# A retention stage in fp32 on one core: three moves in the order of work (low part of the turned values, gate function, scores)

## The reference, cut to what matters

```
q, k = rope(x @ Wq), rope(x @ Wk)          # 8 heads of 128
v, g = x @ Wv, x @ Wg                      # 8 heads of 256
scores = (q * scale) @ k^T * D             # D: decay of the head, causal
o = scores @ v
o = o * rsqrt(mean(o*o) + eps) * g_norm_weight
o = o * silu(g)
x = layernorm(x + o @ Wo)
```

## Time and profile before

| | before |
|---|---|
| median of 3 runs (lowest to highest) | 2827.63 us (2826.35 to 2828.19) |
| the profiled execution: its own time | 2827.04 us |
| its span, first to last instruction | 2825.2 us |
| PE busy | 2757.8 us (98%) |
| DVE busy | 1586.9 us (56%) |
| ACT busy | 1104.8 us (39%) |
| mean granted clock of TensorE | 0.995 |
| PE's share of the chain that ended last | 91% |

### The profile page before, as it was taken

The page is one execution under the profiler, slowest core; times in us unless marked ns, Lnnn a source line. Parts: engine busy times, 40 slices in busy tenths (PEclk is TensorE's granted clock), DMA queues, the critical chain, the costliest instruction groups (busy, mean ns, idle before and its releaser), DMA issues.

```text
span 2825.2 us, 40399 instructions
## 1 busy us (share of the span) xinstructions
PE 2757.8 (98%) x15498; PEld 2506.3 (89%) x15498; DVE 1586.9 (56%) x2104; ACT 1104.8 (39%) x1718; POOL 28.8 (1%) x45
## 2 busy tenths in 40 slices
PE   8999999999999999999989999999999999999997
PEld 7888899888888888888878888889999998998997
DVE  3233222344454444467778888854884573673766
ACT  3333233332223223334457777742442241341432
POOL 0000000000000000000000000000000000000000
PEclk9999999999999999999999999999999999999999
DMA  5222332211111111104112222212211122121222
GB/s 179 84 84 87 102 100 92 84 62 47 58 54 50 45 53 51 60 32 105 60 66 67 72 66 72 66 47 90 79 60 67 55 74 75 53 74 55 75 89 93
DMA packets 88144, 203.51 MB, mean 72 GB/s; under 512 B 9476, under 2 KB 64260, under 8 KB 73832
## 3 DMA queue, kind: packets, MB, share of 16 engines
q1 hardware_dynamic: 88040, 202.09, 21.3%
HBM read 171.86 MB, written 30.21 MB: 72 GB/s over the span
## 4 chain that ended last, share of the span: by engine, by line
PE 91%; DVE 4%; ACT 2%; issue 1%; DMA 0%; SPq 0%; DVEq 0%; POOL 0%; ACTq 0%
PE PS L128 8%; PE PS L130 8%; PE PS L129 8%; PE PS L1957 5%; PE PS L1959 5%; PE PS L1961 5%; PE PS L1482 5%; PE PS L409 3%; PE PS L411 3%; PE PS L410 3%; PE PS L434 3%; PE PS L435 3%; PE PS L436 3%; PE PS L1495 3%; PE PS L1994 2%; PE PS L1993 2%
## 5 line engine op out<-in xcount | busy, mean ns | idle before, releaser
L128 PE MATMUL PS<-XH,WH 128*128 128x512 f32 (+1 forms) x1216 | 423.6, 348 | 4.7 <-ACT G L726 3.8
L130 PE MATMUL PS<-XH,WL 128*128 128x512 f32 (+1 forms) x1216 | 419.8, 345 | 0.0
L129 PE MATMUL PS<-XL,WH 128*128 128x512 f32 (+1 forms) x1088 | 373.7, 343 | 0.0
L88 ACT ACTIVATE WH<-RAW 128x1024 fp32r<-128x1024 f32 x106 | 112.3, 1060 | 499.0 <-PE PS L130 359.5
L94 DVE TENSOR_TENSOR WL<-RAW,WH 128x1024 fp32r<-128x1024 f32 x106 | 129.7, 1224 | 253.0 <-ACT WH L88 251.8
L128 PEld LDWEIGHTS PS<-XH,WH 128*128 128x128 f32 x1216 | 228.8, 188 | 32.2 <-ACT G L726 7.1
L130 PEld LDWEIGHTS PS<-XH,WL 128*128 128x128 f32 x1216 | 228.9, 188 | 25.7
L129 PEld LDWEIGHTS PS<-XL,WH 128*128 128x128 f32 x1088 | 204.5, 188 | 22.5
L2084 ACT ACTIVATE WH<-RAW 128x512 fp32r<-128x512 f32 x180 | 113.4, 631 | 225.7 <-PE PS L1961 118.6
L409 PE MATMUL PS<-CH,KWH 128*128 128x338 f32 (+1 forms) x512 | 168.1, 328 | 13.1 <-DVE CL L385 13.1
L2312 DVE TENSOR_TENSOR WL<-RAW,WH 128x512 fp32r<-128x512 f32 x196 | 134.7, 688 | 61.8 <-ACT WH L2084 59.2
(11 more groups left out here) (311 smaller groups left out, 6582.0 us busy)
## 6 DMA issues: line engine op xcount, KB each, us to landing
RAW<-weights_dram SPq DMA_DIRECT2D x111, 1024.0 KB, 4.9
a_KRAW<-keys_scratch SPq DMA_DIRECT2D x32, 411.0 KB, 3.1
a_VRAW<-values_scratch SPq DMA_DIRECT2D x32, 384.0 KB
R<-context_dram SPq DMA_DIRECT2D x8, 1352.0 KB, 6.8
R<-context_dram SPq DMA_DIRECT2D x7, 1536.0 KB, 7.0
values_scratch<-VS SPq DMA_DIRECT2D x40, 256.0 KB
keys_scratch<-KS SPq DMA_DIRECT2D x8, 768.0 KB, 5.9
keys_scratch<-KS SPq DMA_DIRECT2D x8, 676.0 KB, 5.7
```

What stands on the lines that cost most here:

```text
L128: pe.matmul(out, wh, xh[:, k, cols], start=(k == 0), stop=False)
L129: pe.matmul(out, wh, xl[:, k, cols], start=False, stop=False)
L130: mm = pe.matmul(out, wl, xh[:, k, cols], start=False, stop=(k == KT - 1))
```

## The change

Nothing is computed otherwise and no instruction of an engine is added or removed but register instructions. Three pieces of the order move:

1. Loop heads, DVE: `VL` stood between output additions 3 and 4 (behind a weight split) and now stands behind addition 7. PE's own order in the loop heads stays.
2. Heads 0 to 6, ACT: the gate function of gate unit 1 stood behind the weight split of the second unit of the next head; it now stands ahead of it and waits for `unit_done` itself, at the same count.
3. Heads 0 and 7: PE does the scores ahead of the transposes, and DVE masks the scores ahead of `VL`.

```diff
@@ scalar, head
                 if not end:
-                    weights_ahead(WG + 1, i, first)
+                    u, loop = unit_no(WG + 1, i, first)
+                    act.wait_ge(c.unit_done, 8 * loop + (u + 1 - U_RET))
                 else:
...
                 act.activation(halves(G[:, 1, :]), row800(c, 0), ACT.Silu).then_inc(gated, 1)
                 if end:
                     end_hi(3)
+                else:
+                    weights_ahead(WG + 1, i, first)
                 act.preload_act_table_set("natural_log_exp_and_others")
@@ vector, head
                 if not first and not end:
-                    for n in range(4):
+                    for n in range(KT):
                         add_output(n, i)
-                    weights_ahead(WO, i, first)
...
+                        if n == 3:
+                            weights_ahead(WO, i, first)
+                    turned_low(i)
+                    weights_ahead(WO + 1, i, first)
+                    mask_scores(i)
+                else:
+                    mask_scores(i)
+                    turned_low(i)
                 dve.wait_ge(s_hi, i + 1)
@@ tensor, head
                 if not first and not end:
                     project_output(i, range(4))
+                    turn(i)
                     project_output(i, range(4, KT))
...
                     pe.wait_ge(r_added, 8 * i - 1)
+                    scores(i)
 
                     pe.wait_ge(r_added, 8 * i)
+                else:
+                    scores(i)
+                    turn(i)
```

More of the change, by code:

```diff
@@ L807, in add_last, with turned_low @@
                 norm.add_row(dve, h, n, r_added, 8 * END - 8 + KT * h + n + 1)
-            def head(i, first):
-                end = i is END
-                rope(0, i, first, lambda: weights_ahead(0, i, first))
-                rope(1, i, first, lambda: weights_ahead(1, i, first))
-                for t in range(2):
-                    weights_ahead(WV + t, i, first)
-                if not first and not end:
-                    for n in range(4):
-                        add_output(n, i)
-                    weights_ahead(WO, i, first)
+            def turned_low(i):
                 dve.wait_ge(v_hi, i + 1)
@@ L824, in head, with mask_scores @@
                                   ALU.subtract).then_inc(v_lo, 1)
[L825 to L828, removed]
+            def mask_scores(i):
                 dve.wait_ge(s_raw, i + 1)
@@ L836, in head @@
                 ins.then_inc(s_masked, 1)
+            def head(i, first):
+                end = i is END
+                rope(0, i, first, lambda: weights_ahead(0, i, first))
+                rope(1, i, first, lambda: weights_ahead(1, i, first))
+                for t in range(2):
+                    weights_ahead(WV + t, i, first)
+                if not first and not end:
+                    for n in range(KT):
+                        add_output(n, i)
+                        if n == 3:
[6 more added lines that the diff above has]
+                    turned_low(i)
                 dve.wait_ge(s_hi, i + 1)
@@ L970, in project_last, with turn, scores @@
                     tile(HALF_BANKS[n % 4], 1, n, 1, False, True).then_inc(wo_last, 1)
+            def turn(i):
+                pe.wait_ge(v_kept, 2 * i + 2)
+                for t in range(2):
+                    mm = turn_values(c, pe, VT[:, t, :], 4, t * P, RDV)
+                mm.then_inc(v_turned, 1)
+            def scores(i):
+                pe.wait_ge(qk_lo, 2 * i + 2)
+                for b in range(B):
+                    out = c.PS[0:T, b // 4, (b % 4) * T:(b % 4 + 1) * T]
+                    cols = slice(b * T, (b + 1) * T)
+                    (qh, ql), (kh, kl) = QK
+                    pe.matmul(out, kh[:, cols], qh[:, cols], start=True, stop=False)
+                    pe.matmul(out, kh[:, cols], ql[:, cols], start=False, stop=False)
+                    mm = pe.matmul(out, kl[:, cols], qh[:, cols], start=False, stop=True)
+                mm.then_inc(s_raw, 1)
             def head(i, first):
@@ L1003, in head @@
                     project_output(i, range(4))
[L1005 to L1009, removed]
+                    turn(i)
                     project_output(i, range(4, KT))
-                pe.wait_ge(qk_lo, 2 * i + 2)
-                if not first and not end:
                     pe.wait_ge(r_added, 8 * i - 1)
[L1016 to L1024, removed]
+                    scores(i)
                     pe.wait_ge(r_added, 8 * i)
+                else:
+                    scores(i)
+                    turn(i)
                 weights(WG, i, first)
```

## The result

| | before | after |
|---|---|---|
| median in the comparison (lowest to highest) | 2826.99 us (2824.34 to 2828.19), 4 runs | 2809.47 us (2806.72 to 2811.43), 4 runs |
| ratio, 95% interval | | 0.9938 [0.9926, 0.995] |
| the profiled execution: time, span | 2827.04, 2825.2 us | 2811.43, 2809.6 us |
| PE busy | 2757.8 us | 2757.5 us |
| mean granted clock | 0.995 | 0.993 |

The changed kernel is faster, by 17.5 us where 15.5 were forecast. The median lies 0.03 us under the lower end of the range, 2809.5. The direction and the mechanism came out; the size was too small, and the lower end too near. Of the 2.6 us between the forecast 2812.1 and 2809.47, 2.0 are the larger saving; the other 0.6 is that the kernel before had a median of 2826.99 us in this comparison, where the forecast started from 2827.63.

What follows compares the result with a forecast made beforehand. PE, busy 98% of the span, was taken as the bound, with only its waits to gain. Savings of 6.5 + 4.7 + 4.3 = 15.5 us from 2827.63 gave 2812.1 us, range 2809.5 to 2817.0.

Steps and rivals of the forecast that it cites:

- Bound and mechanism: Whole kernel: PE busy 98% of the span; only its waits can shrink, 12.6 us idle at three places.
- Part 1: Six loop heads: with VL behind the additions, output tiles no longer wait for an addition; 6 x 1.09 = 6.5 us saved.
- The cover of the chain behind it: Loop heads, DVE from addition 7 to SL's end: 3.2 us to spare before PE asks for its results.
- Part 2: Seven head ends: with the gate function ahead of the split, Q starts sooner; 7 x 0.68 = 4.7 us saved.
- the baseline: Head 7: the sums-of-squares matmuls are followed without a wait after 1.45 us, taken as Q's turn at the other head ends.
- the spare time: Head ends: the moved gate function is done 0.4 us ahead of PE's turn for Q.
- Part 3: Heads 0 and 7: scores run inside the transposes' wait for the copy of V; 2 x 2.16 = 4.3 us saved.
- rival (d): Later seam of attention and feed-forward: the clock falls otherwise, 2.6 us either way, 2809.5 or 2814.7; no chance of its own.
- The sum: Whole kernel: 6.5 + 4.7 + 4.3 = 15.5 us saved, giving 2812.1 us, ratio 0.9945.
- (a): Any of the three places: one part gives its wait back to another waiter, 2816.4 to 2818.6 us; one part lost 0.15.
- (b): Six loop heads: VL's late place starves gate unit 1, each microsecond beyond the cover costs 6 us; slower 0.04.
- (c): The three places: register work or issue sets the waits, so no saving, 2827.6 us; within 0.2% 0.05.

Runs made afterwards that it cites:

- cover1: The changed kernel with VL written twice in the six loop heads (one more, about 2.3 us): 2809.4 us, one run.
- cover2: The changed kernel with VL written three times in the six loop heads (two more): 2819.71 us, one run.
- endgate: The changed kernel with head 7's gate function ahead of the third split of the last output weights: second output matmul at 1.52 us instead of 1.70.
- gatelate: The changed kernel with one more ScalarE copy (about 0.43 us) ahead of the gate function at seven head ends: 2813.13 us.
- part 3 alone: The kernel before with only scores ahead of transposes and mask ahead of VL in heads 0 and 7: 2823.24 us, ratio 0.9983.

## Why the prediction was right or wrong

**Bound and mechanism: right.** PE's waits were all there was to gain. All three went, nothing new took their place, and the blocks behind took the saving over.

**Part 1: right to 0.1 us** (6.5 forecast, 6.52 measured alone), with the step from VL's end to addition 4 as its evidence. The cover of the chain behind it was 3.1 us for 3.2 (cover1, cover2).

**Part 2: the mechanism right, the term too small**, 4.7 for 5.76 us. The step that failed is the baseline, "in head 7 the same four are followed without a wait after 1.45 us". They were not: PE's weight load there waited 0.55 us, and the gate function of head 7 held it (endgate). The list of PE's waits did not show it, because PE's matmul row was still counted as busy with the sums of squares; the row of the weight load did. By the second matmul the head 7 baseline was 1.71 us and Q's own is 1.57: 0.14 x 7 = 1.0 us. The row in front of the prediction speaks of four matmuls; the program has two there (line 1057, one for each half of the tokens), which the profile shows as four records. The same error made the spare time 0.4 us instead of 0.15 (gatelate). And a wait may be gone from the list while it still sets the start.

**Part 3: right in its fixed work** (4.3 forecast, 4.19 measured), incomplete in what a wait costs. The step that failed is in rival (d): I looked for falls of the clock only at one later seam where the trace of before had one, and took the wait of 1.93 us in heads 0 and 7 to cost its own length, since that one profile showed the clock at 1.00 there. In two of seven profiles the wait also costs a fall, 4.8 and 1.7 us, about 0.9 us per execution as a mean of these seven. That is a small sample, and part 3 alone took 4.06 us off the median, no more than its fixed work. That falls come behind this wait and cost time is shown; how often they come, and how the length of the wait changes that, is not.

**The sum.** 16.6 us of fixed work, and about 0.9 for falls that no longer come, make 17.5, which is what the comparison gave. With four runs of each, a spread of 4 to 5 us and a share of falls from seven profiles the agreement to 0.1 is luck; in the later sessions the changed kernel was 18.5 and 21.4 us under the kernel before.

**Profile against median.** The prediction had the saving right by the profiled executions (15.6 us) for a wrong reason: 16.6 were saved in the block and 1.0 was lost behind it, in a part of the span that varies from 1641.8 to 1646.6 us between profiles of the same kernel. The range had 2.6 us below the forecast for the clock, from half of one fall in a window of ten microseconds. A mean granted clock of 0.995 over 2825.2 us is some 28 us at the lower level (an estimate: 0.005 x 2825.2 / 0.5), and the part behind the block varied by 4.8 us, so the term was too small in itself; and the range had to hold an error in the sizes and in the starting median as well, and did not.

**The rivals.** (a) no part was lost; the loop's branch costs nothing that shows (part 2 gave 0.83 us per loop head). (b) real, but 3.1 us away. (c) no. (d) true of the later seams, where the term was too small, and missed in head 0.

## What to carry to other kernels

Before a row is taken as "what it costs without a wait", look at the weight load's row as well as the matmul's, and measure to the second matmul behind the place: a matmul that overlaps fp32 work ahead of it can hide a wait of some tenths. A wait of PE of about 2 us can cost more than its length: here 1.93 us cost 1.7 and 4.8 us more in two of seven profiles. One profile with a full clock doesn't show that it always stays up; look at the same place in several. Where an order of work is changed, size the cover of what was moved back by repeating it: one more copy cost nothing, two cost 1.5 us in each head.

## What the runs showed of the hardware

The clock's fall at a given place differs between executions of the same work. With 1.93 us of wait ahead of 1.7 us of transposes it came in 2 of 14 places (seven profiles, two heads each); with 2.69 us in 2 of 2, in one profile that had an early fall as well; with 2.3 and 0.4 us of wait near 550 us in 5 of 17 profiles. Where PE had no wait (nine profiles, heads 0 and 7) it never came. Such falls are one part of the spread of the times, and the seams behind the block are another: that part of the span alone varies from 1641.8 to 1646.9 us over the profiles. And the four records of the sums of squares (two fp32 matmuls of 400 columns), each shown as 0.5 us long and started 0.34 us apart, let the next product's first matmul start 1.09 us after the first of them, with 0.65 us of length of its own.
